# Four GNN layers in one kernel: edge columns turned and edge weights made in pairs, the column numbers cast first, bucket numbers read once per turn

## The reference

```
h = relu(layernorm(x))
for l in range(3):                          # the first GNN: three RGCN layers
    edge_w = edge_attr_32 @ nn_w.T + nn_b   # 50000 x 256, from 32 attributes per edge; the same in each layer
    msg = relu(h[src] * edge_w)
    out = h @ root[l] + bias[l]
    for r in range(3):                      # three edge types
        mean = segment_sum(msg where type == r, dst) / max(count, 1)
        out = out + mean @ W[l, r]
    h = out
x = x + h                                   # then L1 (gated messages), L2 (8 types, attention), L3 (attention)
```

## Time and profile before

| what | before |
|---|---|
| median of three runs | 4750.72 us (4747.5 to 4752.62) |
| profiled execution: span from the first to the last instruction | 4744.9 us |
| busy: PE, PEld, DVE, ACT, POOL | 83%, 68%, 71%, 38%, 65% |
| mean granted TensorE clock | 0.904 |
| layers 0, 1, 2 of the first GNN: first gather to last accumulation | 798.2 to 1350.9, 1437.0 to 1955.4, 2040.8 to 2560.6 us |
| L1271 edge weights (two passes each) | 2358 matmuls, 738.4 us |
| L1263 turning, L1303 copying the columns | 393 of each, 279 and 254 ns each |
| `attT` loads in layers 1 and 2 | 144 KB each |

### The profile page before, as it was taken

The page is one execution under the profiler, slowest core; times in us unless marked ns, Lnnn a source line. Parts: engine busy times, 40 slices in busy tenths (PEclk is TensorE's granted clock), DMA queues, the critical chain, the costliest instruction groups (busy, mean ns, idle before and its releaser), DMA issues. The chain is left out here.

```text
span 4744.9 us, 105920 instructions
## 1 busy us (share of the span) xinstructions
PE 3915.0 (83%) x22300; PEld 3233.3 (68%) x22301; DVE 3382.7 (71%) x9318; ACT 1791.0 (38%) x5399; POOL 3071.7 (65%) x3178
## 2 busy tenths in 40 slices
PE   6799997889987889878899566779978778578886
PEld 3477775778776778767777556668866666366664
DVE  7799997667757778677787667874257778756666
ACT  0355553221123333333333100004257667367774
POOL 0266665777756777567775777766777773067774
PEclk9799998999998999989999777888978898778787
DMA  1233334856626445264452687861465444144445
GB/s 47 92 131 131 130 132 130 212 126 158 152 63 202 135 145 154 71 185 146 145 149 78 208 257 214 245 191 54 145 182 120 105 106 125 32 99 109 109 109 100
DMA packets 643665, 643.00 MB, mean 136 GB/s; under 512 B 314342, under 2 KB 549540, under 8 KB 643396
## 3 DMA queue, kind: packets, MB, share of 16 engines
q0 software_dynamic: 145840, 374.54, 27.8%
q1 hardware_dynamic: 443348, 213.36, 17.0%
q10 hardware_dynamic: 54336, 53.65, 3.3%
HBM read 470.09 MB, written 170.26 MB: 135 GB/s over the span
## 5 line engine op out<-in xcount | busy, mean ns | idle before, releaser
L1059 POOL DMA_INDIRECT G<-h_dram,idx x1572 | 1525.8, 971 | 556.8 <-issue 361.6
L1283 PEld LDWEIGHTS ps_a<-hotm,msg 128*128 128x128 f32 x4716 | 686.5, 193 | 196.2 <-DVE arena L1395 67.5
L1283 PE MATMUL ps_a<-hotm,msg 128*128 128x128 f32 x4716 | 730.0, 282 | 88.5 <-DVE arena L1395 87.8
L1271 PE MATMUL ps_e<-nnw,attT 128*128 128x256 f32 x2358 | 738.4, 396 | 76.8 <-DVE prodm L1388 42.4
L1395 DVE TENSOR_TENSOR arena<-ps_a,arena 128x256 f32 x1404 | 586.9, 418 | 218.8 <-issue 94.1
L735 POOL DMA_INDIRECT rec_dram<-rec,pos x392 | 376.7, 961 | 398.6 <-ACT rec L606 307.7
L1059 POOL DMA_INDIRECT G<-feat_dram,idx x420 | 402.4, 958 | 325.5 <-POOLq L241 197.9
L1317 ACT ACTIVATE msg<-prodm 128x256 f32<-128x256 f32 x786 | 327.5, 417 | 677.8 <-DVE prodm L1388 586.1
L749 POOL DMA_INDIRECT rec_dram<-rows,place x392 | 379.8, 969 | 222.1 <-issue 117.4
L1897 POOL DMA_INDIRECT arena<-rel_dram,idx x393 | 385.0, 980 | 128.6 <-issue 86.2
L1271 PEld LDWEIGHTS ps_e<-nnw,attT 128*128 128x128 f32 x2358 | 370.3, 195 | 118.4 <-DVE prodm L1388 56.4
(11 more groups left out here) (365 smaller groups left out, 7691.6 us busy)
## 6 DMA issues: line engine op xcount, KB each, us to landing
gate<-rec_dram SPq DMA_DIRECT2D x126, 384.0 KB
G<-msg_dram SPq DMA_DIRECT2D x300, 128.0 KB, 2.2
msg_dram<-msg ACTq DMA_DIRECT2D x270, 128.0 KB
rel_dram<-stage SPq DMA_DIRECT2D x25, 1040.0 KB
G<-h_dram,idx POOLq DMA_INDIRECT x1572
aT<-edge_attr SPq DMA_DIRECT2D x98, 128.0 KB
msg_dram<-arena ACTq DMA_DIRECT2D x90, 128.0 KB
attT<-attT_dram SPq DMA_DIRECT2D x74, 144.0 KB
```

Of the source, the lines that this page charges most:

```text
L1059: pool.indirect_dma_start(G[:, n % width, :], None, table, bass.IndirectOffsetOnAxis(ap=idx[:, which, n:n + 1], axis=0)).then_inc(sem(f"sw ...
L1271: t.matmul(ps_e[s % BANKS][:], attT[:, s // HU, s % HU, :], nnw[:], start=True, stop=True).then_inc(sem("ew"), 1)
L1283: last = t.matmul(ps_a[s % BANKS][:, h, :], of[:, h * P:(h + 1) * P], hot[:, s, :], start=True, stop=True)
```

## The change

Two units are turned at once: `att` gets 64 columns per unit, of which column 32 is set to one and 33 to 63 to zero, so that two units side by side are a 128x128 block, and the turned block holds one unit in rows 0 to 32 and the next in rows 64 to 96 (the row of ones carries the bias). `nnw` with its bias stands twice, at rows 0 and 64. The edge weights of a pair are two matmuls of 33 rows, on the two halves, with one signal after the second. Turning and weights happen at odd steps and the step after. In memory `attT_dram` is kept as whole 128-row blocks, in pieces of ten and eight units. `ps_t` is one block instead of two buffers. `begin_rgcn` is gone; `nnw` is loaded in the first block of sorting. In layer 0 the cast of the first column numbers stands ahead of one whole clearing of `arena`. `Buckets` reads 18 numbers once per turn (`part=U`), in the first GNN and in the second.

```
-        attT = sb(ctx, "attT", [P, 2, HU, P])
+        attT = sb(ctx, "attT", [P, HU, P])
...
+HALF = P // 2
+PIECES1 = ((0, HU + 1), (HU + 1, U))
...
+        def ends_pair(c):
+            return c and not c.extra and (c[2] % 2 == 1 or c.late and c[2] == FRONT - 1)
+        def pair_size(c):
+            return c[2] % 2 + 1
...
-                        att = sb(pctx, "att", [P, U, A32]) if l == 0 else None
+                        att = sb(pctx, "att", [P, U, HALF]) if l == 0 else None
-                        ps_t = ps(pctx, "ps_t", [A32, 2, P]) if l == 0 else None
+                        ps_t = ps(pctx, "ps_t", [P, P]) if l == 0 else None
...
+                        for lo in (0, HALF):
+                            sp.dma_start(nnw[lo:lo + A32, :], L0_gnn_nn_w).then_inc(sem("nnw_in"), 16)
+                            sp.dma_start(nnw[lo + A32:lo + A32 + 1, :], L0_gnn_nn_b.rearrange("(a d) -> a d", a=1)).then_inc(sem("nnw_in"), 16)
...
-                begin_rgcn(nnw, attT)
...
-                                        t.transpose(ps_t[:, s % 2, :], att[:, s, :], ident[:]).then_inc(sem("attT"), 1)
-                                    if c1 and not c1.extra:
+                                        pe.wait_ge(sem("attT_sb"), upto(c0.m - pair_size(c0)))
+                                        t.transpose(ps_t[:], att[:, s - s % 2:s - s % 2 + 2, :].rearrange("p s w -> p (s w)"),
+                                                    ident[:]).then_inc(sem("attT"), pair_size(c0))
+                                    if ends_pair(c1):
...
-                                        t.matmul(ps_e[s % BANKS][:], attT[:, s // HU, s % HU, :], nnw[:], start=True, stop=True).then_inc(sem("ew"), 1)
+                                        for k in range(pair_size(c1)):
+                                            rows = slice(k * HALF, k * HALF + A32 + 1)
+                                            last = t.matmul(ps_e[(s - s % 2 + k) % BANKS][:], attT[rows, s // 2, :], nnw[rows, :],
+                                                            start=True, stop=True)
+                                        last.then_inc(sem("ew"), pair_size(c1))
...
-                                            nc.scalar.copy(attT[0:A32, s // HU, s % HU, :], ps_t[:, s % 2, :]).then_inc(sem("attT_sb"), 1)
+                                        nc.scalar.copy(attT[:, s // 2, :], ps_t[:]).then_inc(sem("attT_sb"), pair_size(c0))
...
-                                    v.memset(arena[:, 0:half], 0.0).then_inc(sem("zeroed"), 1)
+                                    v.memset(att[:, :, A32:A32 + 1], 1.0)
+                                    v.memset(att[:, :, A32 + 1:HALF], 0.0).then_inc(sem("atts_set"), 1)
                                     dve.wait_ge(sem("meta_in"), 16)
                                     v.tensor_copy(idx[:, 0, 0:U], meta[:, 0:U, 1]).then_inc(sem("columns"), 1)
-                                    v.memset(arena[:, half:KD * D], 0.0).then_inc(sem("zeroed"), 1)
...
+                                v.memset(arena[:], 0.0).then_inc(sem("zeroed"), 1)
...
-                                bucket = Buckets(nc, mybir.EngineType.DVE, bmap[0:1, 0, :], KD - 1, 8, part=HU)
+                                bucket = Buckets(nc, mybir.EngineType.DVE, bmap[0:1, 0, :], KD - 1, 8, part=U)
...
-                            bucket = Buckets(nc, mybir.EngineType.DVE, bmap[0:1, 1, :], T - 1, 8, part=HU)
+                            bucket = Buckets(nc, mybir.EngineType.DVE, bmap[0:1, 1, :], T - 1, 8, part=U)
```

More of the change, by code:

```diff
@@ L284, in credit, with sort_edges @@
                 eng.sem_inc(sem(name), CREDIT)
-        def sort_edges(nnw, attT):
+        def sort_edges(nnw):
             ctx = ExitStack()
@@ L761, in build @@
         meta2 = arena[:, meta2_at:meta2_at + NC2 * REC2].rearrange("p (n w) -> p n w", n=NC2)
[L764 to L780, removed]
         def empty_pads(sp, empty):
@@ L1294, in _ @@
                                         nc.scalar.copy(tile_h[:], hT[:, ds(i - 1), :, :].rearrange("p t h n -> p (t h n)")).then_inc(sem("tile_h"), 1)
-                                    if c0 and not c0.extra:
+                                    if ends_pair(c0) and l == 0:
                                         n, i, s = c0
[L1297 to L1302, removed]
-                                            nc.scalar.copy(attT[0:A32, s // HU, s % HU, :], ps_t[:, s % 2, :]).then_inc(sem("attT_sb"), 1)
@@ L1304, in _ @@
-                                    if c1 and not c1.extra:
-                                        n, i, s = c1
-                                        if l == 0 and (s % HU == HU - 1 or c1.late and s == FRONT - 1):
-                                            wait_ahead(act, (sem("attT_sb"), upto(c1.m)))
-                                            count = s % HU + 1
-                                            nc.scalar.dma_start(attT_d[:, ds(c1.m - (count - 1), count), :], attT[0:A32, s // HU, 0:count, :]).then_inc(
-                                                sem(f"att_out{s // HU}"), 16)
+                                        act.wait_ge(sem("attT"), upto(c0.m))
@@ new lines, in _ @@
+                                        act.wait_ge(sem("ew"), upto(turn_before(c0)))
+                                        for h, (lo, hi) in enumerate(PIECES1):
+                                            if s - s % 2 == lo and not (isinstance(i, int) and i == 0):
+                                                act.wait_ge(sem(f"att_out{h}"), i * 16)
+                                        nc.scalar.copy(attT[:, s // 2, :], ps_t[:]).then_inc(sem("attT_sb"), pair_size(c0))
+                                    if c1 and l == 0:
+                                        n, i, s = c1
+                                        for h, (lo, hi) in enumerate(PIECES1):
+                                            if s == (min(hi, FRONT) if c1.late else hi) - 1:
+                                                wait_ahead(act, (sem("attT_sb"), upto(c1.m)))
+                                                pairs = slice(lo // 2, s // 2 + 1)
+                                                nc.scalar.dma_start(attT_d[:, ds(i * HU + lo // 2, s // 2 + 1 - lo // 2), :], attT[:, pairs, :]).then_inc(
+                                                    sem(f"att_out{h}"), 16)
@@ L2433, in build @@
             nnw = sb(ctx, "nnw", [P, D])
-            attT = sb(ctx, "attT", [P, 2, HU, P])
-            sort_edges(nnw, attT)
+            attT = sb(ctx, "attT", [P, HU, P])
+            sort_edges(nnw)
             rgcn(nnw, attT)
```

37 lines of the change are left out of this document (20 added, 17 removed).

## The result

The changed kernel takes 4962 us (median; 4951 to 4986), the kernel before 4752: ratio 1.045 (95% interval 1.042 to 1.048). The forecast was 4705. In the profiled executions the span went from 4744.9 to 4969.6 us, mean clock from 0.904 to 0.851.

| stretch, us | before | after | difference |
|---|---|---|---|
| up to layer 0's first one-hots | 807.9 | 807.6 | -0.3 |
| first twelve turns of layers 0 / 1 / 2 | 274.7 / 248.2 / 248.2 | 296.7 / 272.8 / 262.2 | +60.6 |
| thirteen late turns of layers 0 / 1 / 2 | 243.8 / 227.1 / 228.4 | 267.9 / 284.1 / 283.0 | +135.8 |
| last turn of layers 0 and 1 to the next layer's first | 258.7 | 280.6 | +21.9 |
| from layer 2's last turn on | 2207.8 | 2214.5 | +6.7 |

What follows compares the result with a forecast made beforehand. Full turns were taken as bound by POOL's gathers, late turns as slower than POOL, PE busiest. Late turns 31 us, (a) 6.6, (b) 6 and last turns about 1 took the span from 4744.9 to 4700, median 4705; range 4678 to 4738.

Steps and rivals of the forecast that it cites:

- (f): Late turns: PE idles in the long read, clock halves after every second one, costing 0.44 us a turn.
- (e): Bucket reads of 18 once a turn: short and hidden every second turn, else 3.1 us, adding 2.2 us.
- (c): Edge weights in pairs on PE: two half-array matmuls overlap, a pair costs 0.64 to 0.66 us against 0.88.
- (a): Before sorting: the block clearing `nnw` and `attT` goes, gaining 6.6 us.
- (b): Layer 0's start: cast of column numbers ahead of most clearing, first gather 5.6 to 7.5 us sooner, taken as 6.
- (d): Layer 0: turning in pairs saves PE about 0.11 us a pair, but 0.15 us of waiting is charged.
- Rival 2: Slower: halves don't overlap, a pair costs 1.08 us, late turns grow, 4773 us; chance 0.07.
- Rival 3: No change: late-turn reads of 4.1 us with half clock after each, 4744 us; chance 0.14.

Runs made afterwards that it cites:

- Aligned nines: Late turns read nine bucket numbers from a copy aligned to 16 bytes: kernel before 4691 us, changed kernel 4876 us, changed kernel with 64 rows 4732 us.
- the step of slack: Pairs on 64 rows with 16-byte-aligned reads of nine (4732 us), with ACT's and DVE's work on a unit and its aggregation one step later: 4745 us.
- the clearing on POOL: Kernel before with 16-byte-aligned reads of nine (4691 us), weight-clearing block dropped, its clearing on POOL, first cast ahead of clearing `arena`: 4694 us.

## Why the prediction was wrong

The step that failed is **(f)**, the clock, and with it the claim ahead of it that full turns are POOL's and untouched. Half clock after every second long read, for 3.5 us of work, was put at 0.44 us a turn and only in late turns. In layer 1 four of the six long turns between turns 12 and 25 ran at half clock for over 20 us and took 29.3 us instead of 21.6; the first twelve turns of the three layers lost 61 us. Mending the rows alone takes 119 us off (4962 to 4843). The earlier trace rows showed a recovery within 4 us, but with 128-row matmuls; the change replaced them by 33-row ones, and I carried the recovery over. With 64 rows it holds. That it is the rows is shown by four pairs of runs that differ in them, and in the clearing that more rows need, alone: 4962 and 4843, 5034 and 4841, 4876 and 4732, and, with lone matmuls, 5326 or 5382 and 5036 us. Why the rows bear on the clock is not shown, nor what numbers between 33 and 64 would do.

**(e)** was mis-sized: 3.1 us taken, 4.07 measured, the upper bound "twice nine". The middle rested on nine and ten costing the same, but in the earlier trace rows the nine are DVE's and the ten SP's; on one engine ten cost 0.22 us more than nine, and the third group of up to eight, for which a microsecond was added, showed in no run. The short read isn't hidden either: 1.57 us leave DVE 0.64 us idle at 1834.27, since the one-hots cover 1.28. Aligned nines instead of 18 take another 111 us off (4843 to 4732). That half the reads are short, and that late turns alternate, was right; by 4 us, not 2.

**(c)** had the mechanism right: two halves start together and a pair takes 0.63 us to the next aggregation. The saving isn't there, since I charged the change of mode 0.20 us a pair. With 64 rows PE's order is

```profile
1737.84 0.70 PE L1288 MATMUL ps_e<-nnw,attT 64*128 64x256 f32 x4
1738.47 1.16 PE L1302 MATMUL ps_a<-hotm,G 128*128 128x128 f32 x8
1739.56 0.70 PE L1288 MATMUL ps_e<-nnw,attT 64*128 64x256 f32 x4
```

1.72 us for two units against twice 0.88: of 1.72, 0.43 are the pair's columns and 0.88 the aggregations', and 0.41 is what the two changes add. The first pass behind a change takes 0.1 us longer too (0.21 us to the next start, where later ones take 0.11): the earlier trace rows already had that, with 0.38 us for the first two passes of `ps_z` and 0.28 for the last two. A thirteenth, lone unit pays the same, so a late turn's PE work doesn't shrink: 18 times 0.44, seven groups of 0.84 and the root matmul, which takes 0.9 us and not the 0.44 I counted, are 14.7 us, against 14.5 for 31 lone ones and the root. Beside it DVE waits 1.6 us a turn for edge weights, with aligned nines and 64 rows, against 0.4 us in the lone order. So pairs cost 37 us (4732 against 4694) where the forecast had them win. Which part of those 37 is DVE's wait is open, since the step of slack moved the wait without ending it.

**(a) and (b)** came about as priced where they stand, and reached nothing. The block's gap shrinks from 10.35 us (161.39 to 171.74) to 4.29, 6.1 gained of 6.6; but the block ahead ends 2.7 us later, 2.2 us with the clearing on POOL (163.62), so the sorting loop starts 3.4 us sooner, at 168.39 and not near 165. That the loading of `nnw` does this wasn't tried. The first gather comes 4.84 us after its column numbers are asked for instead of 10.71: 5.9 us sooner. But DVE's clearing, now in one piece, starts 3.95 us behind the cast, and the first one-hots come at 807.6 us as before; the gathers start 20 us ahead of that and then wait for their 18 buffers. The sentence "as the full turns are POOL's, this reaches the start of the late turns whole" is what failed. **(d)** held: with clock 1.00 layer 0's late turns are 1.0 us longer than layer 1's (17.8 and 16.8 us), 0.9 forecast. The second GNN's accumulations span 498.4 us (2896.5 to 3394.9) against 499.3 (2675.2 to 3174.5), inside the bounds, and the doubled columns cost nothing that shows: the first twelve turns with 64 rows and reads of 18 take 270, 251 and 251 us, before 275, 248 and 248.

Rival 2, the slower one, had the right side by a wrong mechanism: its pairs cost 1.08 us. Rival 3 had the read right, 4.1 us with half clock behind each, and came to 4744 us, since it carried the short recovery over as well.

## To carry to other kernels

A pause costs what it lasts plus what the engine does at the lower clock, and how long that is depends on the matmuls that follow: with half-filled ones look for rows at granted clock 0.50 with PE busy throughout, and fill the rows of both halves up, with zeros if need be. One half alone stayed low even with 64 rows. Price a change of array mode by the period of the whole pattern, not by the gap in front of one instruction. Put tables that an engine reads number by number at multiples of 16 bytes: here that alone took 61 us off the kernel before.

## Unexpected in the hardware

- A pair on 33 rows of each half and one on 64 (with zeros) take the same 0.63 us, but after a pause of 4.18 us PE is back at 2.4 GHz within 4 us with 64 rows and still at 1.2 GHz after 20 us with 33.
- Lone matmuls on 33 rows lose the clock without a pause: PE is busy throughout, and of each full turn of 37.6 us it works 30.7 at 1.2 GHz.
- Eight useless 128-row matmuls a turn made the changed kernel 106 us faster.
- A read of 12 numbers at a multiple of 16 bytes takes 0.79 us, 4 bytes further 2.59 us.
